# Attention values with the exponentials stationary and nine columns of v moving

## The chip, the cores and the metric

The kernel runs on one core of a Trainium2 chip. The metric is the device time of one launch in microseconds; the times given are of whole executions, and one further execution was profiled.

The engines are named as in the profile: PE is TensorE's matmul, PEld its load of the stationary operand, DVE is VectorE, ACT is ScalarE, POOL is GpSimd, SP is SyncE, which issues the DMAs.

## What is computed

Two layers run over 4 sequences of 1024 tokens with 128 features. The part that matters here is the attention of the second layer's gate branch (16 heads of 8 features, all 1024 tokens as queries and as keys):

```python
NUM_HEADS = 16                      # hd = 128 // 16 = 8
qkv = (x @ W_qkv + b_qkv).reshape(B, S, 3, H, hd)
q, k, v = (qkv[:, :, 0], qkv[:, :, 1], qkv[:, :, 2])
attn = jnp.einsum('bqhd,bkhd->bhqk', q, k) / jnp.sqrt(jnp.asarray(hd, x.dtype))
attn = jax.nn.softmax(attn, axis=-1)
attn_out = jnp.einsum('bhqk,bkhd->bqhd', attn, v).reshape(B, S, D)
...
return attn_out + moe_out
```

Beside it stand a gated feed-forward layer, a second kind of attention with a recurrence over time, a mixture of 8 experts, layer norms and a residual sum. In the kernel much of that is done in the gaps of the loop that is described next.

## The kernel before

There is one program for all engines, without loops at run time: everything is unrolled, and the order on each engine is the order in the code. Engines wait for each other through counted signals (`wait_ge`; `up` adds one). Some weights are handled by other code if they are not exactly representable; that code stands in the program and is jumped over (`t_br_lt`, `t_br`).

For each of the 4 sequences the kernel first does the first layer, then projects queries, keys and values, then runs the attention loop of `CYCLES` = 67 cycles. The loop goes over `QUADS` = 64 quads: 4 groups of four heads (`g4`), 2 halves of the queries (`c`, 512 queries each) and 8 blocks of 128 keys (`jt`, the innermost). In cycle `k_`

- PE makes the scores of quad `k_` (`m_scores`): for each of the four heads one product with 128 keys as the stationary side and 512 queries as the moving side, into four of six PSUM banks in turn;
- ACT turns them into exponentials, two heads at a time (line 1064), into `prob`, a ring of 12 slots of 512 columns in the buffer `big`. The softmax takes no maximum over the row (a bound is computed once instead);
- PE makes the values of quad `k_ - 2` (`m_values`): for each of the four heads the stationary side is `vaug`, 128 keys by 32 columns (8 features of v, a column of ones whose product is the softmax's sum, and 23 columns that belong to other heads and aren't used), the moving side the exponentials of 512 queries. The four products go to the four groups of 32 columns of the PE array and of 32 partitions in `ACC_BANK`, and are summed over the eight key blocks. The result has features in rows and queries in columns;
- PE, and after it DVE, ACT or POOL, do one side piece from the table `SIDE`: parts of the other branches. All side pieces share one PSUM bank, `SIDE_BANK`, so each waits until the one before has been read (`side_free`).

After each eighth value quad `copy_out` (DVE, line 739) copies `ACC_BANK` to `oT` in SBUF, and sets `oT_ok`, for which the values of the next eight quads wait. A side piece "nat" then transposes it on PE (four transposes of 128 x 128, line 1527) so that tokens are in rows, and `attention_out` (DVE) takes the reciprocal of the sums (line 746) and multiplies (line 748) into `att`. The last "nat", of quads 56 to 63, comes after the last values of the sequence; the sums with the experts' result (POOL, line 913), a silu (ACT, line 1099), two more operations on POOL and the store wait for it.

PE's products all have one source line, 1105 (the helper `mm`), so they are told apart by their tiles: `ps<-big,vaug` are the values, `ps<-hid` the scores, `ps<-wo_sb,qz` the side piece "o", an output projection with 32 stationary and 128 moving columns.

Of the kernel before, what the change touches and what calls it, by code (L numbers as in the profile page):

```python
# [21 lines left out]
P = 128  # L22
B, S, D = 4, 1024, 128
NT = S // P
CH = 512
# [6 lines left out]
GH = 4  # L32
# [24 lines left out]
NAT_LAST_BANK = 0  # L57
# [63 lines left out]
def build_program(nc, x, fw, lw, aw, wo, cst, cols, rows, bexp, out):  # L121
    with ExitStack() as ctx:
# [6 lines left out]
        def sig(name, per=1, start=0, left_out=0):  # L129
            return Signal(ctx, nc, name, per, start, left_out)  # L130
# [62 lines left out]
        oT = [wk[:, i * CH:(i + 1) * CH] for i in range(2)]  # L193
# [64 lines left out]
        mp_mm, oT_ok = sig("mp_mm", QUADS), sig("oT_ok", 2 * NG, 1)  # L258
        oN_mm, att_ok = sig("oN_mm", 2 * NG), sig("att_ok", 2 * NG, 1)
# [110 lines left out]
        def _(v):  # L370
# [67 lines left out]
            for b in range(B):  # L438
# [295 lines left out]
                def copy_out(n_):  # L734

                    v.wait_ge(mp_mm.sem, mp_mm.at(b, (n_ + 1) * NT))
# [25 lines left out]
                for k_ in range(CYCLES):  # L762
                    if k_ >= LAG and (k_ - LAG) % NT == NT - 1:
                        copy_out((k_ - LAG) // NT)
# [12 lines left out]
                    elif what == "nat":  # L777
                        attention_out(i)
# [145 lines left out]
        def _(a):  # L924
# [7 lines left out]
            for s_ in (chain, wblk_used, msum_ok, fin_ok, stored, z_ok, oT_ok, att_ok):  # L932
                a.sem_inc(s_.sem, s_.start)
# [169 lines left out]
        def _(t_):  # L1103
# [47 lines left out]
            for b in range(B):  # L1151
# [20 lines left out]
                t_.wait_ge(oT_ok.sem, oT_ok.at(b, 0))  # L1172
# [267 lines left out]
                def m_values(k_):  # L1440
# [7 lines left out]
                    if jt == 0 and k_:  # L1448
                        t_.wait_ge(oT_ok.sem, oT_ok.at(b, k_ // NT))
# [8 lines left out]
                def side_free(k_):  # L1458
# [5 lines left out]
                    elif what == "nat":  # L1464
                        t_.wait_ge(att_ok.sem, att_ok.at(b, i + 1))
# [19 lines left out]
                for k_ in range(CYCLES):  # L1485
# [36 lines left out]
                    elif what == "nat":  # L1522
                        side_free(k_)
                        t_.wait_ge(oT_ok.sem, oT_ok.at(b, i + 1))
# [162 lines left out]
```

## Time and profile before

| | |
|---|---|
| median of 3 runs | 1012.39 us (1012.34 to 1013.4) |
| the profiled execution | 1012.52 us, its span 1010.7 us |
| granted TensorE clock, mean | 0.996 |
| PE busy | 960.6 us, 6930 matmuls and as many loads |
| ACT busy | 746.0 us |
| DVE busy | 547.9 us |
| POOL busy | 198.5 us |
| the four attention loops | 147.1, 148.0, 148.3 and 144.7 us |

Busy time is the time in which an engine has at least one instruction under way, so four matmuls side by side count once. The end of a matmul is modelled by the profiler, its start is recorded. The loops are the stretches from 124.3, 367.1, 610.7 and 854.6 us on. The instruction queues in the profile's list of DMA queues are those over which the engines' own code arrives; q8 is PE's, as the next to last group of rows below is read.

### The profile page before, as it was taken

To read this page: it belongs to the slowest core of one execution; us is meant where nothing else is said; L and a number is where in the kernel's file an instruction comes from. 1 tells how busy PE (TensorE), PEld (TensorE's weight loads), DVE (VectorE), ACT (ScalarE), POOL (GpSimd) and SP (SyncE) were. 2 spreads that over 40 slices of the span, in tenths; PEclk is the share of its full clock that TensorE was granted. 3 is DMA by queue.
4 is the path that set the end of the run, shared out by engine and by line. 5 is a ranking of instruction groups with operands and counts; after the bars stand their busy time and mean duration, and the time that the engine had idled before them with its cause. 6 is when DMAs were issued, how large, how long until landed. Compare 5 with 4: busy or idle time off the path is not lost.

```text
span 1010.7 us, 17808 instructions
## 1 busy us (share of the span) xinstructions
PE 960.6 (95%) x6930; PEld 536.1 (53%) x6930; DVE 547.9 (54%) x1336; ACT 746.0 (74%) x914; POOL 198.5 (20%) x145
## 2 busy tenths in 40 slices
PE   3999999999899999999989999999999999999995
PEld 2888633343488853334358874334437886333431
DVE  6655735645556654554565574456447556346262
ACT  5543699989763479998956359998985446999885
POOL 1200202412300020441130020233212002035023
PEclk9999999999999999999999999999999999999998
DMA  6000133000000023200000012310000002320000
GB/s 249 1 1 1 24 48 62 1 3 1 1 22 1 2 39 50 43 2 2 1 22 1 1 17 43 51 24 2 2 1 22 1 1 26 51 35 2 2 1 23
DMA packets 17625, 22.18 MB, mean 22 GB/s; under 512 B 2976, under 2 KB 14336, under 8 KB 17280
## 3 DMA queue, kind: packets, MB, share of 16 engines
q1 hardware_dynamic: 17536, 20.99, 10.3%
q8 instruction: 57, 0.93, 0.4%
q14 instruction: 32, 0.26, 0.1%
HBM read 7.85 MB, written 2.10 MB: 10 GB/s over the span
## 4 chain that ended last, share of the span: by engine, by line
PE 76%; DVE 8%; ACT 7%; issue 6%; POOL 2%; DMA 0%; POOLq 0%; DVEq 0%; ACTq 0%
PE ps L1105 73%; ACT big L1064 3%; PE ps L1527 2%; DVE st L279 1%; ACT xn L1036 1%; DVE wk L563 1%; DVE wk L739 1%; ACT spl L1017 1%; ACT qz L1012 1%; DVE flags L420 1%; PE ps L1125 1%; DVE xn L452 1%; POOL st L877 1%; PE ps L1520 0%; DVE spl L460 0%
## 5 line engine op out<-in xcount | busy, mean ns | idle before, releaser
L1064 ACT ACTIVATE big<-ps 128x1024 f32<-128x1024 f32 x512 | 493.6, 1034 | 40.2 <-PE ps L1105 38.2
L1105 PE MATMUL ps<-big,vaug 128*32 128x512 f32 x2048 | 272.6, 604 | 3.6 <-DVE wk L739 2.3
L1105 PE MATMUL ps<-hid 32*128 32x512 f32 x1024 | 130.5, 493 | 4.3 <-ACT big L1064 2.9
L1105 PE MATMUL ps<-hid,fw_sb 128*128 128x512 f32 x416 | 101.2, 397 | 0.3 <-DVE hid L468 0.3
L980 ACT ACTIVATE wk<-ps,cols_sb 128x512 f32<-128x512 f32 x64 | 40.6, 687 | 80.2 <-PE ps L1105 74.4
L877 POOL TENSOR_TENSOR st<-st 128x4 f32<-128x4 f32 x16 | 16.2, 1010 | 389.0 <-DVE st L552 287.5
L1105 PEld LDWEIGHTS ps<-hid 32*128 32x128 f32 x1024 | 49.3, 181 | 81.5 <-issue 50.6
L891 POOL TENSOR_TENSOR qz<-qz,wk 128x512 f32<-128x512 f32 x32 | 41.2, 1288 | 244.0 <-DVE wk L709 244.0
L1105 PEld LDWEIGHTS ps<-hid,fw_sb 128*128 128x128 f32 x416 | 77.5, 188 | 18.5 <-DVE hid L468 1.1
L1105 PEld LDWEIGHTS ps<-big,vaug 128*32 128x32 f32 x2048 | 41.0, 108 | 69.6 <-issue 35.2
L727 DVE SCALAR_TENSOR_TENSOR big<-ps,sm,big 128x128 f32<-128x128 f32 x128 | 44.3, 346 | 47.0 <-PE ps L1105 35.8
L1105 PEld LDWEIGHTS ps<-wk,big 128*128 128x128 f32 x512 | 60.8, 191 | 2.1
L1105 PE MATMUL ps<-wk,big 128*128 128x129 f32 x512 | 61.0, 274 | 0.0
L1105 PE MATMUL ps<-xt_hi,lw_hi 128*128 128x512 f32 x112 | 50.7, 452 | 5.4 <-DVE wk L563 4.5
L1105 PEld LDWEIGHTS ps<-lw_hi,xt_hi 128*128 128x128 f32 x96 | 18.0, 188 | 62.4 <-DVE wk L727 34.1
L970 ACT ACTIVATE wk<-ps,cols_sb 128x512 f32<-128x512 f32 x32 | 21.9, 689 | 36.6 <-PE ps L1105 36.6
L1105 PEld LDWEIGHTS ps<-xt_hi,lw_hi 128*128 128x128 f32 x112 | 20.9, 187 | 47.9 <-issue 8.2
L696 DVE TENSOR_SCALAR wk<-ps,decay 128x512 f32<-128x512 f32 x32 | 25.9, 809 | 36.6 <-PE ps L1105 36.1
L468 DVE TENSOR_TENSOR hid<-wk,hid 128x512 fp32r<-128x512 f32 x64 | 44.3, 692 | 2.2
L1105 PE MATMUL ps<-xt_hi,lw_lo 128*128 128x512 f32 x112 | 44.2, 395 | 0.0
L466 DVE CAST hid<-wk 128x512 fp32r<-128x512 f32 x64 | 27.1, 423 | 31.6 <-ACT wk L980 30.2
L1105 PE MATMUL ps<-xt_lo,lw_hi 128*128 128x512 f32 x112 | 43.1, 396 | 0.1
(215 smaller groups left out, 1577.8 us busy)
## 6 DMA issues: line engine op xcount, KB each, us to landing
hid<-spl SPq DMA_DIRECT2D x288, 32.0 KB
xnext<-in_x SPq DMA_DIRECT2D x4, 512.0 KB, 4.0
out<-qz SPq DMA_DIRECT2D x8, 256.0 KB, 2.3
big<-in_fw SPq DMA_DIRECT2D x1, 1877.0 KB, 9.3
hid<-one_row SPq DMA_DIRECT2D x16, 96.0 KB
wk<-in_lw SPq DMA_DIRECT2D x1, 1476.0 KB, 14.2
big<-in_fw SPq DMA_DIRECT2D x1, 939.0 KB, 11.1
cst_sb<-in_cst SPq DMA_DIRECT2D x1, 440.0 KB, 4.4
```

The costliest lines, as they stand in the source:

```text
L279: step(v.bn_stats(bn[:, t, :], src[:, t, :]))
L466: up(hid_hi, v.tensor_copy(hidden(buf, 0, m), src))
L468: up(hid_lo, v.tensor_tensor(hidden(buf, 1, m), src, hidden(buf, 0, m).bitcast(F32), ALU.subtract))
L696: up(v_copy, v.tensor_scalar(v1[u % 4], ps[:, SIDE_BANK, :], decay[:, KM + m:KM + m + 1], decay[:, 2 * KM + m:2 * KM + m + 1], ALU.mult, A ...
L727: ins = v.scalar_tensor_tensor(acc, src, weight, acc, ALU.mult, ALU.add)
L877: up(rstd_ok, g_.tensor_tensor(rstd[:, tl], var[:, tl], half[:, tl], ALU.pow))
L891: up(qs_ok, g_.tensor_tensor(qz[:, m, sl], qz[:, m, sl], v1[u % 4], ALU.mult))
L970: up(l1_act, a.activation(act32[n_ % 3], ps[:, L1_BANKS[c][m % 2], :], ACT.Silu, scale=col("w1s", m)))
L980: up(h_act, a.activation(act32[n_ % 3], ps[:, banks[m], :], ACT.Gelu, scale=col(name, m)))
L1064: up(ms_exp, a.activation(prob[:, at:at + 2 * CH].rearrange("p (h n) -> p h n", n=CH), ps[:, bank:bank + 2, :], ACT.Exp, scale=HDM ** -0.5))
L1105: return t_.matmul(out_, lhsT, rhs, start=start, stop=stop, **kw)
L1527: ins = t_.transpose(ps[:, bank, q * P:(q + 1) * P], oT[i % 2][:, q * P:(q + 1) * P], ident)
```

## The change

The sides of the value product are swapped. The stationary side is now 32 queries' exponentials (128 keys by 32 columns), the moving side 9 columns of `vaug` (8 features and the ones). One quad has 4 blocks of 128 queries, 4 heads and, within a block, 4 groups of 32 queries, which go to the four column groups: 64 products where there were 4. The result lies in `ACC_BANK` with tokens in rows already, 16 pieces of 9 columns. So `copy_out`, `oT`, the eight "nat" pieces of each sequence and their bank go; `attention_out` reads `ACC_BANK` itself, at the place in DVE's order where the copy was, and what waited for `oT_ok` now waits for `att_ok`. Since the 16 pieces of a bank can't each start their own sum, four products of 32 x 144 with a stationary side of zeros set the bank to zero ahead of each eight quads.

```diff
-                    for g in range(GH):
-                        at, w = ((GH * k_ + g) % RING) * CH, (jt * HM + g4 * GH + g) * (HDM + 1)
-                        ins = mm(ps[QUAD * g:QUAD * (g + 1), ACC_BANK, :], vaug[:, w:w + QUAD], prob[:, at:at + CH],
-                                 jt == 0, jt == NT - 1)
+                        t_.wait_ge(att_ok.sem, att_ok.at(b, k_ // NT))
+                    if jt == 0:
+                        for g in range(GH):
+                            mm(ps[QUAD * g:QUAD * (g + 1), ACC_BANK, 0:TPC * GH * (HDM + 1)], vaug[:, NT * HM * (HDM + 1):],
+                               vaug[:, 0:TPC * GH * (HDM + 1)], True, False)
+                    for q in range(TPC):
+                        for h in range(GH):
+                            w, to = (jt * HM + g4 * GH + h) * (HDM + 1), (q * GH + h) * (HDM + 1)
+                            for g in range(GH):
+                                at = (GH * k_ + h) % RING * CH + q * P + QUAD * g
+                                ins = mm(ps[QUAD * g:QUAD * (g + 1), ACC_BANK, to:to + HDM + 1], prob[:, at:at + QUAD],
+                                         vaug[:, w:w + HDM + 1], False, jt == NT - 1 and q == TPC - 1 and h == GH - 1)
...
-                def copy_out(n_):
+                def attention_out(n_):
+
+                    g4, c = n_ // NCH, n_ % NCH
                     v.wait_ge(mp_mm.sem, mp_mm.at(b, (n_ + 1) * NT))
-                    if n_ == 0:
-                        v.wait_ge(hsT_mm.sem, hsT_mm.at(b, 2))
-                    up(oT_ok, v.tensor_copy(oT[n_ % 2], ps[:, ACC_BANK, :]))
-
-                def attention_out(n_):
-
-                    g4, c = n_ // NCH, n_ % NCH
-                    v.wait_ge(oN_mm.sem, oN_mm.at(b, n_ + 1))
-                    oN = ps[:, NAT_LAST_BANK if n_ == 2 * NG - 1 else SIDE_BANK, :].rearrange("p (i n) -> p i n", n=QUAD)
+                    oN = ps[:, ACC_BANK, 0:TPC * GH * (HDM + 1)].rearrange("p (i n) -> p i n", n=HDM + 1)
                     step(v.reciprocal(rec, oN[:, :, HDM]))
...
-                    elif what == "nat":
-                        side_free(k_)
-                        t_.wait_ge(oT_ok.sem, oT_ok.at(b, i + 1))
-                        bank = NAT_LAST_BANK if i == 2 * NG - 1 else SIDE_BANK
-                        for q in range(TPC):
-                            ins = t_.transpose(ps[:, bank, q * P:(q + 1) * P], oT[i % 2][:, q * P:(q + 1) * P], ident)
-                        up(oN_mm, ins)
```

On PE, around the first "nat" of a sequence (`hid` are the scores, rows with `vaug` the values, `xt_hi,lw_hi` and its like a side piece); before:

```order
L1105 MATMUL ps<-hid 128x512 x4
L1105 MATMUL ps<-big,vaug 32x512 x4
L1527 MATMUL ps<-cst_sb,wk 128x128 x4
L1105 MATMUL ps<-hid 128x512 x4
L1105 MATMUL ps<-big,vaug 32x512 x4
```

and now:

```order
L1093 MATMUL ps<-hid 128x512 x4
L1093 MATMUL ps<-vaug 32x144 x4
L1093 MATMUL ps<-vaug,big 32x9 x64
L1093 MATMUL ps<-xt_hi,lw_hi 128x512
L1093 MATMUL ps<-xt_lo,lw_hi 128x512
L1093 MATMUL ps<-xt_hi,lw_lo 128x512
L1093 MATMUL ps<-hid 128x512 x4
L1093 MATMUL ps<-vaug,big 32x9 x64
L1093 MATMUL ps<-hid 128x512 x4
```

The transposes are gone and nothing has taken their place in the table; each row of four value products has become one of 64. (PE takes each product of two float32 operands in two passes, each a load and a matmul.)

On DVE, at the first end of eight quads; before, the copy stands ahead of a side piece, and reciprocal and product follow three and more instructions later:

```order
L666 COPY sm<-ps 128x32
L739 COPY wk<-ps 128x512
L666 COPY sm<-ps 128x32
L647 TENSOR_REDUCE sm<-sm 128x8
L649 TENSOR_TENSOR sm<-sm 128x64
L696 TENSOR_SCALAR wk<-ps,decay 128x512
L746 RECIPROCAL cst_sb<-ps 128x16
L748 TENSOR_TENSOR big<-ps,cst_sb 128x4x32
```

and now both stand where the copy was:

```order
L663 COPY sm<-ps 128x32
L736 RECIPROCAL cst_sb<-ps 128x16
L738 TENSOR_TENSOR big<-ps,cst_sb 128x4x32
L663 COPY sm<-ps 128x32
L644 TENSOR_REDUCE sm<-sm 128x8
L646 TENSOR_TENSOR sm<-sm 128x64
L693 TENSOR_SCALAR wk<-ps,decay 128x512
```

The copy of 512 columns has left DVE, and the next eight quads' values wait for the product instead of for it.

## Rows read from the trace of the kernel before

**Rows 1.** The page: busy time of each engine, share of the span, instructions.

```profile
PE 960.6 (95%) x6930; PEld 536.1 (53%) x6930; DVE 547.9 (54%) x1336; ACT 746.0 (74%) x914; POOL 198.5 (20%) x145
```

**Rows 2.** Busy time by stretch (us): the four attention loops, then what lies around.

```profile
core 0: us, PE busy (x) PEld busy (x) DVE busy (x) ACT busy (x) POOL busy (x), PEclk, DMA share, GB/s
124.30:271.40 147.10, 143.91 (x1238) 55.34 (x1238) 71.50 (x196) 135.51 (x157) 33.59 (x24) 1.00 0.12 21
...
854.60:999.30 144.70, 140.89 (x1224) 53.70 (x1224) 67.01 (x176) 131.95 (x146) 31.92 (x23) 1.00 0.11 18
sum 588.10, PE 572.81 PEld 219.83 DVE 282.23 ACT 539.52 POOL 132.68; mean PE 143.20 PEld 54.96 DVE 70.56 ACT 134.88 POOL 33.17
...
999.30:1010.70 11.40, 0.63 (x4) 0.42 (x4) 1.24 (x3) 1.42 (x3) 6.22 (x5) 0.63 0.18 50
sum 422.60, PE 387.75 PEld 316.29 DVE 265.69 ACT 206.43 POOL 65.86; mean PE 77.55 PEld 63.26 DVE 53.14 ACT 41.29 POOL 13.17
```

**Rows 3.** Groups by form: count, busy us, mean ns of one, idle before and releasers.

```profile
L1064 ACT ACTIVATE big<-ps 128x1024 f32<-128x1024 f32 x512 | 493.6, 1034 | 40.2 <-PE ps L1105 38.2
L1105 PE MATMUL ps<-big,vaug 128*32 128x512 f32 x2048 | 272.6, 604 | 3.6 <-DVE wk L739 2.3 <-ACT big L1064 0.4
L1527 PE MATMUL ps<-cst_sb,wk 128*128 128x128 f32 x128 | 20.9, 286 | 4.7 <-DVE wk L739 4.7
L739 DVE COPY wk<-ps 128x512 f32<-128x512 f32 x32 | 21.9, 685 | 20.8 <-PE ps L1105 20.8
L748 DVE TENSOR_TENSOR big<-ps,cst_sb 128x128 f32<-128x128 f32 x32 | 9.3, 292 | 1.1
L746 DVE RECIPROCAL cst_sb<-ps 128x16 f32<-128x16 f32 x32 | 8.1, 254 | 25.3 <-PE ps L1527 25.3
```

**Rows 4.** Timeline of PE in the first loop: start us, us, what, count.

```profile
206.76 1.06 PE L1105 MATMUL ps<-wo_sb,qz 128*32 128x128 f32 x32
207.74 0.50 PE L1105 MATMUL ps<-hid 32*128 32x512 f32 x4
208.17 1.06 PE L1105 MATMUL ps<-big,vaug 128*32 128x512 f32 x8
209.06 1.06 PE L1105 MATMUL ps<-wo_sb,qz 128*32 128x128 f32 x32
210.04 0.51 PE L1105 MATMUL ps<-hid 32*128 32x512 f32 x4
210.48 1.07 PE L1105 MATMUL ps<-big,vaug 128*32 128x512 f32 x8
211.36 1.06 PE L1105 MATMUL ps<-wo_sb,qz 128*32 128x128 f32 x32
```

**Rows 5.** The value products by tile: duration ns min/median/max, first and last start.

```profile
L1105 PEld LDWEIGHTS ps<-big,vaug x2048: 105/108/111, 129.4 to 998.3; 128*32 128x32 f32 x187
L1105 PE MATMUL ps<-big,vaug x2048: 589/593/619, 129.4 to 998.7; 128*32 128x512 f32 x187
```

**Rows 6.** Timeline of PE's loads, one value burst.

```profile
182.53 0.19 PEld L1105 LDWEIGHTS ps<-big,vaug 128*32 128x32 f32 x8 [0.50 <-issue]
```

**Rows 7.** PE's instruction queue over the span; then DMAs from 1000.5 to 1006.5.

```profile
q8 instruction: 57, 0.93, 0.4%
...
DMA  0000040000001000000000000006100000000005
GB/s 0 0 0 0 0 109 0 0 0 0 0 0 55 0 0 0 0 0 0 0 0 0 0 0 0 0 0 109 55 0 0 0 0 0 0 0 0 0 0 154
...
q8 instruction: 2, 0.03, 2.7%
```

**Rows 8.** Timeline of all engines after the last values.

```profile
999.41 0.69 DVE L739 COPY wk<-ps 128x512 f32<-128x512 f32 x1 [6.16 <-PE ps L1105]
999.47 0.63 ACT L1099 ACTIVATE qz<-big 128x512 f32<-128x512 f32 x1
1000.22 0.42 PEld L1527 LDWEIGHTS ps<-cst_sb,wk 128*128 128x128 f32 x4 [1.85 <-issue]
1000.25 0.63 PE L1527 MATMUL ps<-cst_sb,wk 128*128 128x128 f32 x4 [0.97 <-DVE wk L739]
1000.92 0.26 DVE L746 RECIPROCAL cst_sb<-ps 128x16 f32<-128x16 f32 x1 [0.81 <-PE ps L1527]
1001.21 0.29 DVE L748 TENSOR_TENSOR big<-ps,cst_sb 128x128 f32<-128x128 f32 x1
1001.58 1.26 POOL L913 TENSOR_TENSOR big<-big 128x512 f32<-128x512 f32 x1 [4.51 <-DVE big L748]
```

More of the change, by code:

```diff
@@ L56 @@
 NORM_BANK, BOUND_BANK, VALUES_BANKS = 0, 3, (7, 7, 7)
-NAT_LAST_BANK = 0
 HEAD_ROWS = (slice(64, 80), slice(96, 112))
 SIDE = {0: ("qk", 5), 1: ("qk", 6), 2: ("mv", 1), 3: ("q", 7), 4: ("mv", 2), 5: ("k", 7), 6: ("hs", 0), 7: ("hs", 1),
[8 rows of a table removed]
[8 rows of a table added]
 CYCLES = QUADS + LAG + 1
@@ L192, in build_program @@
         moe2 = wk[:, S:2 * S].rearrange("p (t d) -> p t d", d=D)
-        oT = [wk[:, i * CH:(i + 1) * CH] for i in range(2)]
         late = cst_sb[:, CSEL:CSEL + 4 * P]
@@ L257, in build_program @@
         ms_mm, ms_exp = sig("ms_mm", 2 * QUADS), sig("ms_exp", 2 * QUADS)
-        mp_mm, oT_ok = sig("mp_mm", QUADS), sig("oT_ok", 2 * NG, 1)
-        oN_mm, att_ok = sig("oN_mm", 2 * NG), sig("att_ok", 2 * NG, 1)
+        mp_mm, att_ok = sig("mp_mm", QUADS), sig("att_ok", 2 * NG, 1)
         comb_ok, cT_mm, cT_ok, eb_mm = sig("comb_ok"), sig("cT_mm"), sig("cT_ok"), sig("eb_mm", 2)
@@ L732, in experts @@
                     v.wait_ge(ex_ok.sem, ex_ok.at(b, i + 1))
-                def copy_out(n_):
-                    v.wait_ge(mp_mm.sem, mp_mm.at(b, (n_ + 1) * NT))
-                    if n_ == 0:
-                        v.wait_ge(hsT_mm.sem, hsT_mm.at(b, 2))
-                    up(oT_ok, v.tensor_copy(oT[n_ % 2], ps[:, ACC_BANK, :]))
                 def attention_out(n_):
                     g4, c = n_ // NCH, n_ % NCH
-                    v.wait_ge(oN_mm.sem, oN_mm.at(b, n_ + 1))
-                    oN = ps[:, NAT_LAST_BANK if n_ == 2 * NG - 1 else SIDE_BANK, :].rearrange("p (i n) -> p i n", n=QUAD)
+                    v.wait_ge(mp_mm.sem, mp_mm.at(b, (n_ + 1) * NT))
+                    oN = ps[:, ACC_BANK, 0:TPC * GH * (HDM + 1)].rearrange("p (i n) -> p i n", n=HDM + 1)
                     step(v.reciprocal(rec, oN[:, :, HDM]))
@@ L763, in _ @@
                     if k_ >= LAG and (k_ - LAG) % NT == NT - 1:
-                        copy_out((k_ - LAG) // NT)
+                        attention_out((k_ - LAG) // NT)
                     what, i = side_piece(b, k_)
@@ L776, in _ @@
                             softmax8_shift(w3d(6), 0, 1, hs_sub)
-                    elif what == "nat":
-                        attention_out(i)
                     elif what == "v":
@@ L930, in normalise_next @@
                 ins.then_inc(signal, 1)
-            for s_ in (chain, wblk_used, msum_ok, fin_ok, stored, z_ok, oT_ok, att_ok):
+            for s_ in (chain, wblk_used, msum_ok, fin_ok, stored, z_ok, att_ok):
                 a.sem_inc(s_.sem, s_.start)
@@ L1171, in _ @@
                 row_scores(0)
-                t_.wait_ge(oT_ok.sem, oT_ok.at(b, 0))
+                t_.wait_ge(att_ok.sem, att_ok.at(b, 0))
                 t_.wait_ge(r_lo.sem, r_lo.at(b, 0))
@@ L1448, in m_values @@
                     if jt == 0 and k_:
-                        t_.wait_ge(oT_ok.sem, oT_ok.at(b, k_ // NT))
-                    for g in range(GH):
-                        at, w = ((GH * k_ + g) % RING) * CH, (jt * HM + g4 * GH + g) * (HDM + 1)
-                        ins = mm(ps[QUAD * g:QUAD * (g + 1), ACC_BANK, :], vaug[:, w:w + QUAD], prob[:, at:at + CH],
-                                 jt == 0, jt == NT - 1)
+                        t_.wait_ge(att_ok.sem, att_ok.at(b, k_ // NT))
[10 more added lines that the diff above has]
+                                         vaug[:, w:w + HDM + 1], False, jt == NT - 1 and q == TPC - 1 and h == GH - 1)
                     up(mp_mm, ins)
@@ L1463, in side_free @@
                         t_.wait_ge(head_in.sem, head_in.at(b, 2))
-                    elif what == "nat":
-                        t_.wait_ge(att_ok.sem, att_ok.at(b, i + 1))
                     elif what == "v":
@@ L1521, in _ @@
                         up(hs_mm, ins)
-                    elif what == "nat":
-                        side_free(k_)
-                        t_.wait_ge(oT_ok.sem, oT_ok.at(b, i + 1))
-                        bank = NAT_LAST_BANK if i == 2 * NG - 1 else SIDE_BANK
-                        for q in range(TPC):
-                            ins = t_.transpose(ps[:, bank, q * P:(q + 1) * P], oT[i % 2][:, q * P:(q + 1) * P], ident)
-                        up(oN_mm, ins)
                     elif what == "v":
```

16 rows, old and new, of the table SIDE are left out of this document.

## Prediction

> **What bounds the kernel now.** I read the page's busy shares first: PE 960.6 us (95%), ACT 746.0 us (74%), DVE 54% [rows 1]. A busy PE need not be a full one, so I cut the span into stages. Four stretches of 144.7 to 148.3 us, 588.1 us in sum, are the attention loops, one per sequence; the 422.6 us around them hold little that the change touches [rows 2]. A loop has 64 cycles with scores, so a cycle takes 588.1 / 256 = 2.30 us. In a cycle ACT makes two exponentials of 1034 ns [rows 3], 2.07 us, which leaves it 0.23 us. PE does the four score products, the values of the quad two cycles back, and a side piece. The timeline shows a cycle with no gap on PE: scores start at 207.74, values at 208.17, the side piece at 209.06, the next scores at 210.04 [rows 4]. So scores take 0.43 us, values 0.89 us, this side piece 0.98 us. PE ends last in most cycles, ACT is close behind.
>
> The profile counts 2048 value matmuls [rows 3], 8 per cycle for 4 in the code: a float32 product is a load and a matmul twice over. Its four column groups run side by side: the 8 matmuls of 604 ns each need 0.89 us, not 4.8.
>
> **The change, part by part.**
>
> 1. *The values.* The code now issues 64 products per cycle, each with 32 stationary and 9 moving columns. At two passes that is 128 loads and 128 matmuls, 256 instructions, where there were 16. What one such pair costs the trace doesn't show; it bounds it.
>  - *By columns.* Each group's pass of 512 columns takes 0.89 / 2 = 0.445 us, so 9 columns take some 8 ns: nothing.
>  - *By loads.* The first matmul of a value burst lasts 619 ns where its own load is exposed and 593 where it was hidden [rows 5]: 26 ns for 32 stationary columns. The four groups load side by side: eight loads of 108 ns begin and end within 0.19 us [rows 6]. So four pairs cost 26 ns if the next load hides under the running matmul, 26 + 8 = 34 if not. A cycle has 32 such fours: 0.83 to 1.09 us. Against 0.89 that is -0.06 to +0.20 us a cycle.
>  - *By pairs.* The nearest dense stream is the output projection (stationary 32 columns, moving 128): 32 pairs in 0.98 us [rows 4], 30.6 ns a pair. If that is the price of a pair whatever it moves, a cycle pays 128 x 30.6 = 3.92 us, +3.03.
>  - *By supply.* The cycles from 206.76 to 211.36 [rows 4] issue 88 loads and matmuls in 2.30 us, 26 ns each, sustained; the burst of [rows 6] shows the 8th load, the 15th instruction, 0.08 us behind the first, under 6 ns each, though these may have stood in a queue. Instructions come to PE in blocks by DMA: 57 packets of 16 KB on its instruction queue for 13,860 loads and matmuls [rows 1, 7], some 250 to a block (two of the 57 come after the jump below). How fast can blocks come? Only one place has PE in need of one: after its last matmul, at 1000.88, PE jumps over code that wasn't run to the program's end. In the DMA strip of that stretch (0.15 us to a slice) a block arrives in slice 5, at 1001.25, and the next in slice 27, at 1004.55: 3.3 us apart, though one takes 1.3 us to move (2.7% of 16 engines over 6.0 us, two packets) [rows 7]. It looks as if the second is not asked for until the first is in use. If a loop is fed like that, one block in hand while the next is fetched, it gets 250 instructions per 3.3 us.
>
>    A loop now has 1238 loads and as many matmuls [rows 2]; take off 1024 of the values and 56 of the transposes, add 16,384 and 128: 17,908, or 71 blocks. At 3.3 us that is 234 us per loop, 937 for four, where 588.1 stand: **+349 us**. I take this one: it is the only row that shows what happens when PE has to wait for code, and 3.66 us per cycle lies between the other bounds (2.2 and 5.3). The sustained 26 ns would give 7.3 us a cycle, but the work set that pace. Ends: if restarting after the jump is 0.7 us of the 3.3, 2.6 us a block and 738 us, +150; at 3.7, 1051 us, +463.
>
>    The Trainium skill, "Runtime: NRT & Kernel Launch", section Instruction fetch mechanics, has the sequencer fetch one 16 KiB page while it runs the current one, and holds that this hides under an issue floor of about 20 cycles per instruction; it also gives PE a memory of 2048 instructions. The 3.3 us between blocks speak for one page ahead. The floor, 17 ns if its cycles are those of 1.2 GHz, would make the 280 instructions of a cycle 4.7 us and the kernel 1610 us by an estimate; the 15 within 0.08 us don't bear it out.
>
> 2. *Clearing the bank.* Once per eight cycles four products of 144 zero columns: by the pass above 2 x 144 / 512 x 0.445 = 0.25 us, 8 per loop, 2.0 us of PE. In a loop that waits for code it hides; only in the array-bound rival does it count.
>
> 3. *Copy, transposes, their waits.* Gone are 32 copies of 685 ns on DVE and 128 transposes on PE [rows 3]. The last set of four is busy 0.63 us [rows 8], 0.29 of it the last one's own length [rows 3], so they start 0.11 us apart: 0.45 us of PE per set, seven sets per loop, 13 us in all. Like part 2 this is hidden where code is waited for. The freed bank: the next column of cycles may start its values once reciprocal (254 ns) and product (292 ns) are done, 0.55 us, where it waited for the copy, 0.69. PE's value matmuls waited 2.3 us in all for that [rows 3], so it is worth nothing. DVE has room (54%).
>
> 4. *The end of a loop.* The last copy starts at 999.41, the reciprocal at 1000.92 [rows 8]; now the reciprocal starts where the copy did, 1.51 us earlier, on the way to the sums and the store. Four times: **-6 us**.
>
> 5. *Other queues.* SP issues the same DMAs. ACT reuses a slot of the exponentials' ring once its values are done, so it falls back with PE and costs nothing itself.
>
> **Sum.** The profiled execution took 1012.52 us (span 1010.7), 0.13 above the median of 1012.39. 1012.5 + 349 - 6 = **1355 us**.
>
> **The rivals.**
>
> *A. Code arrives in time and the loads hide: faster.* The point is the price of a block: below 250 / 280 x 2.2 = 2.0 us the supply no longer sets the cycle. For it: the 1.3 us that a block takes to move, and the burst's 6 ns. Against: 3.3 us. With 26 ns per four pairs: values -0.06 x 256 = -15, clearing +8, transposes -13, ends -6: **987 us**. ACT stops this early, since 2.07 us of a cycle's 2.30 are its own; nearer 995.
>
> *B. The same, but the load stands open.* +0.20 x 256 = 51, and 8 - 13 - 6: 1052 us. At 6 ns for each of 256 instructions, none of them ready beforehand, the values take 1.54 us, and it is 1168 us. So 1015 to 1170.
>
> *C. A price per pair.* 30.6 ns each: 1012.5 + 3.03 x 256 - 6 = **1782 us**. For it: no stream in this profile goes faster for long. Against: that one moves 128 columns per product, and its four groups' time of 0.11 us is just what 128 columns cost by the 0.445 us of 512. The Trainium skill, "TensorE: Matmul & The Clock Gate", section Wait — 56ns, not 53.3ns?, states that starts of matmuls never come closer than about 25 ns however little they move. An estimate by it: 128 x 25 ns = 3.2 us of values per cycle, 1598 us. In four column groups the rows above show starts closer than that, but only in short bursts.
>
> *D. Forecast's cause, and the clock falls.* PE would stream little in 3.66 us. The granted clock is 1.00 in every loop and 0.63 only where PE stands idle at the end [rows 2]. At half speed scores (0.86), values (32 x 52 ns = 1.66) and a side piece (1.96) would make 4.5 us a cycle, above 3.66: +0.8 x 256, 1570 us at most, less where the side piece is short.
>
> **How the numbers follow.** Supply by blocks, the clock high or low (1150 to 1570): 0.45, likeliest 1355. A price per pair or per matmul (1590 to 1790): 0.20. B: 0.20. A, or within 2 us of before: 0.08. The rest, 0.07, is slower still or between the cases. About 0.2%, 2 us, is what a measurement can tell from no change here: faster 0.06, same 0.02, slower 0.92. The range leaves out A, the lower half of B and the upper part of C: 1060 to 1700.
>
> **What would show it.** Supply: cycles of 3.3 to 4 us, PE's waits put down to issue, gaps every 250 instructions, blocks on the instruction queue 3.3 us apart through the whole loop, some 300 in all. C: gaps spread evenly, starts 25 to 31 ns apart, blocks further apart than they need be. B: cycles near 2.5 us. A: values of 0.83 us and ACT without idle time. D: a granted clock near 0.5 in the loops. It would be wrong at the root if PE keeps several blocks in flight, or if the 3.3 us belong to the jump alone.

## The result: half as long again, and TensorE waiting for its own code

| | before | after |
|---|---|---|
| median | 1012.51 us (1012.34 to 1013.4) | 1492.22 us (1485.06 to 1497.16) |
| the profiled execution, its span | 1012.52, 1010.7 us | 1497.16, 1495.4 us |
| granted TensorE clock, mean | 0.996 | 0.753 |
| the four attention loops | 588.1 us [rows 2] | 1066.4 us |
| packets on PE's instruction queue | 57 [rows 7] | 297 |

The ratio of after to before is 1.473 (95%: 1.468 to 1.478). First the page of after: the busy times that answer to [rows 1], the strips of PE and of its clock over 40 slices of the span, the instruction queue, and the three costliest groups by line, which answer to [rows 3] (busy us, mean ns of one, idle time before them and what ended it).

```profile
PE 1297.0 (87%) x37778; PEld 981.9 (66%) x37778; DVE 530.4 (35%) x1304; ACT 755.2 (51%) x914; POOL 197.1 (13%) x145
...
PE   5998898778999898877999988998789997887785
...
PEclk9998655786799755578679976557768997657775
...
q8 instruction: 297, 4.87, 1.4%
...
L1052 ACT ACTIVATE big<-ps 128x1024 f32<-128x1024 f32 x512 | 495.8, 1022 | 458.0 <-PE ps L1093 455.6
L1093 PEld LDWEIGHTS ps<-vaug,big 128*32 128x32 f32 x32768 | 431.1, 138 | 237.6 <-issue 230.5
L1093 PE MATMUL ps<-vaug,big 128*32 128x9 f32 x32768 | 465.3, 194 | 135.8 <-issue 134.7
```

PE issues 37,778 pairs where it issued 6930. ACT does the same work as before (495.8 us of exponentials) but now stands idle for 458 us in front of it, waiting for PE. And PE waits too, for nothing that another engine does: "issue" is time in which the profile shows no cause. The view of waits adds these up (us in total, times, longest):

```profile
PEld ps L1093 <- issue: 385.4, 616, 2.8
...
PE ps L1093 <- issue: 162.3, 167, 2.6
```

Busy time by stretch shows where the 484.6 us between the two profiled executions lie. These are three of the four loops of after, from the first scores to the last values (the third, from 854.01, takes 266.24 us); the sum of all four answers to that of [rows 2].

```profile
124.56:388.63 264.07, 223.41 (x8953) 161.93 (x8954) 67.90 (x189) 138.41 (x157) 33.25 (x24) 0.69 0.08 15
485.40:754.28 268.88, 228.47 (x8953) 166.54 (x8954) 68.25 (x189) 139.93 (x159) 33.26 (x24) 0.66 0.08 15
...
1218.09:1485.26 267.17, 216.07 (x8940) 159.45 (x8940) 62.86 (x169) 134.59 (x147) 31.64 (x23) 0.69 0.08 13
sum 1066.36, PE 897.62 PEld 655.45 DVE 267.29 ACT 552.62 POOL 131.41; mean PE 224.41 PEld 163.86 DVE 66.82 ACT 138.16 POOL 32.85
```

A cycle now takes 1066.4 / 256 = 4.17 us. What lies around the loops takes 1495.4 - 1066.4 = 429.0 us, where the same cut through before (first scores to last values, each loop 0.6 us shorter at most than in [rows 2]) leaves 425.0. So +480.6 us in the loops, +4.0 around them.

What a single wait looks like stands in PE's timeline (start us, us, what, count, idle before), here in the first loop:

```profile
157.02 0.51 PE L1093 MATMUL ps<-hid 32*128 32x512 f32 x4
157.46 0.98 PE L1093 MATMUL ps<-vaug,big 128*32 128x9 f32 x94
160.11 0.66 PE L1093 MATMUL ps<-vaug,big 128*32 128x9 f32 x34 [1.68 <-issue]
160.70 1.12 PE L1513 MATMUL ps<-cst_sb,xn 128*128 128x128 f32 x4
161.74 0.80 PE L1093 MATMUL ps<-hid 32*128 32x512 f32 x4
```

The 128 value matmuls of one cycle break after the 94th, in the middle of a group of four, and go on 1.68 us later. No semaphore stands there, and 94 of them took only 0.98 us. In the record of the instruction queue a block of code starts to move at 157.15 and is in at 158.60; PE's first matmul behind it starts at 160.11. In each loop 69 such blocks arrive, one every 264.1 / 69 = 3.83 to 268.9 / 69 = 3.90 us; for the first loop the list of queues has (packets, MB, share of 16 engines)

```profile
q8 instruction: 69, 1.13, 1.8%
```

Within one block, four pairs of load and matmul for the four column groups start 30 to 31 ns apart at the full clock (2.4 GHz) and 52 to 53 ns apart at the half (1.2 GHz), so a cycle's 128 pairs would need 1.0 us, against the 0.89 of before.

So the reading before any experiment: the array could do the new values nearly as fast as the old ones, but the code for them doesn't arrive.

### The profile page after: what moved, and what is told of

The parts are those of the page before. It is cut to its first block, busy times and chain, and to the rows that moved or that the text cites. A ratio compares the mean times of both kernels' runs of the same rounds, so it can differ in the third digit from the quotient of the medians.

```text
span 1495.4 us, 79426 instructions
## 1 busy us (share of the span) xinstructions
PE 1297.0 (87%) x37778; PEld 981.9 (66%) x37778; DVE 530.4 (35%) x1304; ACT 755.2 (51%) x914; POOL 197.1 (13%) x145
## 4 chain that ended last, share of the span: by engine, by line
PE 80%; issue 14%; DVE 3%; ACT 2%; POOL 1%; DMA 0%; POOLq 0%; DVEq 0%
PE ps L1093 78%; DVE wk L560 1%; PE ps L1513 0%; ACT spl L1005 0%; ACT qz L1000 0%; DVE st L276 0%; DVE flags L417 0%; PE ps L1113 0%; PE ps L1567 0%; DMA xnext<-in_x 0%; DVE xres L507 0%; DVE wk L502 0%; ACT qz L916 0%; DVE hid L465 0%; POOL big L901 0%
## 5 line engine op out<-in xcount | busy, mean ns | idle before, releaser
L1052 ACT ACTIVATE big<-ps 128x1024 f32<-128x1024 f32 x512 | 495.8, 1022 | 458.0 <-PE ps L1093 455.6
L1093 PEld LDWEIGHTS ps<-vaug,big 128*32 128x32 f32 x32768 | 431.1, 138 | 237.6 <-issue 230.5
L1093 PE MATMUL ps<-vaug,big 128*32 128x9 f32 x32768 | 465.3, 194 | 135.8 <-issue 134.7
L1093 PE MATMUL ps<-hid 32*128 32x512 f32 x1024 | 188.3, 664 | 5.5 <-issue 5.0
L1093 PEld LDWEIGHTS ps<-hid 32*128 32x128 f32 x1024 | 71.1, 242 | 109.3 <-issue 103.4
L968 ACT ACTIVATE wk<-ps,cols_sb 128x512 f32<-128x512 f32 x64 | 40.5, 687 | 80.2 <-PE ps L1093 74.4
L1093 PE MATMUL ps<-wo_sb,qz 128*32 128x128 f32 x1024 | 50.7, 341 | 16.6 <-issue 16.6
L1093 PE MATMUL ps<-xt_hi,lw_hi 128*128 128x512 f32 x112 | 59.5, 531 | 4.9 <-DVE wk L560 4.5
L1093 PE MATMUL ps<-lw_hi,xt_hi 128*128 128x512 f32 (+1 forms) x96 | 53.0, 552 | 2.2 <-issue 2.2
L1093 PE MATMUL ps<-xt_lo,lw_hi 128*128 128x512 f32 x112 | 50.2, 459 | 1.5 <-issue 1.4
L1093 PEld LDWEIGHTS ps<-wo_sb,qz 128*32 128x32 f32 x1024 | 38.1, 138 | 17.0 <-issue 16.7
```

The lines of the kernel that those rows point to most:

```text
L968: up(h_act, a.activation(act32[n_ % 3], ps[:, banks[m], :], ACT.Gelu, scale=col(name, m)))
L1052: up(ms_exp, a.activation(prob[:, at:at + 2 * CH].rearrange("p (h n) -> p h n", n=CH), ps[:, bank:bank + 2, :], ACT.Exp, scale=HDM ** -0.5))
L1093: return t_.matmul(out_, lhsT, rhs, start=start, stop=stop, **kw)
```

## The experiments

The theory: in code that runs straight through, PE (its loads and matmuls together) is handed a block of 256 instructions every 3.4 to 3.9 us whatever is in it, and the number of instructions sets the time. The rivals: a price of each pair of load and matmul (25 to 31 ns, C), and the fallen clock (D).

**Fewer products.** e1_half computes the values of two of the four heads, e2_threeq those of three (the softmax's sums of the others are replaced, so the output isn't the attention's):

```diff
-                        for h in range(GH):
+                        for h in range(2):        # e2_threeq: range(3)
...
-                    step(v.reciprocal(rec, oN[:, :, HDM]))
+                    step(v.reciprocal(rec, (oN[:, 0:1, HDM]).broadcast_to([P, TPC * GH])))
```

> Leaves out the value products of two of each group's four heads (their outputs are wrong), so a quad has 32 products instead of 64. Supply theory (a block of 256 PE instructions every 3.85 us, whatever is in it): a loop has 17,931 - 8192 = 9739 instructions, 38 blocks, 147 us of supply; that is no longer above what PE and ACT need, so the loops fall to 147 to 160 us and the kernel to 1000 to 1060 us, with few waits put down to issue. Price per pair (each load and matmul costs the same everywhere): the values of the changed kernel cost 1492 - 1012 + 228 = 708 us in all, half of them go, 1138 us. Clock theory (the halved clock is what costs): as the price per pair.

> Leaves out one of each group's four heads (wrong outputs), 48 products to a quad. Supply: 17,931 - 4096 = 13,835 instructions per loop, 54 blocks at 3.85 us = 208 us where 266.5 stand, 1492 - 4 x 58 = 1259 us, blocks still 3.7 to 3.9 us apart. Price per pair: a quarter of 708 us goes, 1315 us, and the blocks come further apart only as the work asks. The two kernels with fewer products together: by supply the first quarter is worth 233 us and the second 200 to 260; by price both 177.

Measured: 1064.92 and 1288.79 us. The first lies 5 us above what supply expected and 73 below the price per pair, the second in the middle of the two. Counted by loops: in e1_half 37 or 38 blocks arrive in 156.7 to 163.3 us, 4.2 to 4.4 us apart, further apart than in after, so code is no longer the only limit there (a cycle is 2.5 us, near the 2.3 that ACT and PE need in any case). In e2_threeq 53 blocks come in 212 to 221 us, 4.0 to 4.2 apart. But the size of the step speaks for nobody: the third quarter of the products costs 224 us and the last 203, for 8192 pairs each, 27 and 25 ns a pair. A price per pair of 25 ns would explain those two numbers just as well. It needed other runs.

**More columns per product.** e3_wide32 moves 32 columns of v where after moves 9; the number of instructions is the same (the clearing of the bank is 64 columns wider too, and the overlap of the columns spoils the output):

```diff
-                                ins = mm(ps[QUAD * g:QUAD * (g + 1), ACC_BANK, to:to + HDM + 1], prob[:, at:at + QUAD],
-                                         vaug[:, w:w + HDM + 1], ...
+                                ins = mm(ps[QUAD * g:QUAD * (g + 1), ACC_BANK, to:to + 32], prob[:, at:at + QUAD],
+                                         vaug[:, w:w + 32], ...
```

> All 64 products, but each moves 32 columns instead of 9 (sums are wrong where they overlap): the same number of instructions, 3.6 times the columns. Supply: the same time, 1480 to 1510 us, since four pairs then cost at most 30 to 60 ns, still below what a block's wait allows. Clock theory: the granted clock rises above 0.75 with more columns streamed, and the time falls with it, by 50 us or more. Price per column: slower, by 23 x 64 x 256 x 2 passes at the half clock, over 100 us.

Measured: 1487.96 us, at a granted clock of 0.917 where after has 0.753. The strip of the clock, PE's waits over the span (162.3 us of this kind in after), and the timeline of a stretch in the first loop:

```profile
PEclk9999888889999999999999998899979998888896
...
PE ps L1093 <- issue: 297.5, 239, 2.6
```

```profile
203.01 1.20 PE L1093 MATMUL ps<-vaug,big 128*32 128x32 f32 x116
205.83 0.32 PE L1093 MATMUL ps<-vaug,big 128*32 128x32 f32 x12 [1.62 <-issue]
```

The clock rises and the time stays within 0.3%: the loops take 266.0 to 269.3 us, 69 blocks each. Over the four loops PE is busy for 761.5 us where after has 897.6: what the work got back from the clock became waiting. In the stretch shown 116 matmuls run in 1.20 us and then PE waits 1.62. At the half clock the same stretch of after has only a short wait, since the work fills the time between two blocks:

```profile
205.85 1.78 PE L1093 MATMUL ps<-vaug,big 128*32 128x9 f32 x116
207.90 0.39 PE L1093 MATMUL ps<-vaug,big 128*32 128x9 f32 x12 [0.27 <-issue]
```

So the clock is a consequence here and not a cause; what it takes from the work it takes from the wait.

**The operations by themselves.** e4_micro is a kernel of its own that does none of the reference's work: long streams of products of one form, with no other engine in the loop. The forms are, in this order, 9 moving columns in float32, 128 columns in float32, 9 columns with 128 stationary ones, 9 columns in bfloat16 (one pass, so no second load), then a loop at run time whose body is 112 pairs of load and matmul, and last 9 columns in one column group alone.

> No layer at all, the output is the input: PE alone runs streams of products one after the other, with nothing to wait for. First 32 of 128 x 200 (to wake the clock), then 512 float32 products of 32 stationary and 9 moving columns in four column groups (2048 instructions, 8 blocks), 512 with 128 moving columns, 96 with 128 stationary and 9 moving, 1024 bfloat16 ones of 32 and 9 (one pass each, 2048 instructions), then a loop at run time of 56 such float32 products (10 columns, 224 instructions) run 16 times, and 256 in one column group alone. Supply: every straight stream that needs a block in less than about 3.4 us gets one each 3.3 to 3.8 us, so the 9-column stream takes 27 to 30 us and the bfloat16 one the same; inside a block four pairs take 30 ns (60 at the half clock); the loop at run time, whose code is already there, runs at that pace throughout, 16 x 112 pairs in 14 us (28 at the half clock), and no block arrives in it. Price per pair: loop and straight code alike, evenly spaced, 25 to 31 ns a pair.

Its timeline of PE, with lines of each form:

```profile
30.66 1.25 PE L158 MATMUL ps<-va,pr 128*32 128x9 f32 x128 [2.19 <-issue]
34.11 1.89 PE L158 MATMUL ps<-va,pr 128*32 128x9 f32 x128 [2.21 <-issue]
37.56 1.89 PE L158 MATMUL ps<-va,pr 128*32 128x9 f32 x128 [1.56 <-issue]
41.29 1.90 PE L158 MATMUL ps<-va,pr 128*32 128x9 f32 x128 [1.84 <-issue]
...
67.12 3.72 PE L158 MATMUL ps<-va,pr 128*32 128x128 f32 x128 [0.29 <-issue]
...
131.48 1.19 PE L158 MATMUL ps<-vab,prb 128*32 128x9 bf16 x128 [2.26 <-issue]
135.21 1.19 PE L158 MATMUL ps<-vab,prb 128*32 128x9 bf16 x128 [2.54 <-issue]
...
153.66 53.82 PE L158 MATMUL ps<-va,pr 128*32 128x10 f32 x2211 [2.38 <-issue]
```

Bursts of exactly 128 matmuls, which with their loads are 256 instructions, begin 3.45 or 3.73 us apart. Whether a burst is busy for 1.25 us (full clock) or 1.89 us (half), in float32 or bfloat16, the next begins at the same distance. The 128-column stream, whose 128 matmuls are busy for 3.72 us, hardly waits (0.29 us). The last row is the loop (1697 of the 2211 matmuls, until 179.0 us) and the stream in one column group behind it, without a break between. From the third on, the loop's 16 passes of 112 pairs take 1.66 to 1.67 us each, 14.9 ns a pair at the half clock. A last block moves over the instruction queue from 156.24 to 157.20 us, and then none until 184.66: the last 13 passes run without one. Nearly the same pairs (10 columns for 9) that cost 27 ns each in straight code (3.45 / 128) cost 15 in a loop. That is what a price per pair can't do: 27 ns is the spacing of blocks divided by 128.

The starts in this trace also show why a block's content doesn't matter as long as it is short. For all 14 bursts that begin behind a wait, a transfer takes 0.88 to 1.30 us, PE's first matmul follows 1.25 to 1.54 us after its end, and the next transfer begins 1.03 to 1.20 us after that matmul. The three add up to the 3.45 or 3.73 us from burst to burst. So the next block isn't asked for until the one before is in use, as the prediction had guessed from two blocks.

**The same products with less code.** In e5_loop 48 of a cycle's 64 value products are three passes of a loop at run time over the same 16, in the kernel itself (constant addresses, and the reciprocal as in e1_half, so the output isn't the attention's):

```diff
-                    for q in range(TPC):
+                    def block_of(q, last):
                         for h in range(GH):
...
+                        return ins
+
+                    with t_.Fori(0, TPC - 1):
+                        block_of(0, False)
+                    ins = block_of(TPC - 1, jt == NT - 1)
```

> PE executes the same 64 products a quad, but 48 of them come from a loop at run time: the 16 products of the first 128 queries are run three times, the last 16 once (the middle two blocks' sums are therefore wrong). Executed loads and matmuls as in the changed kernel, plus three branches; code to fetch about 155 instructions a cycle instead of 280. Supply theory: 0.62 blocks of 3.85 us is 2.4 us a cycle, so the work itself sets the pace: scores 0.43, values 32 x 31 ns and three branches of 0.21, a side piece of 0.9, 3.0 us a cycle at full clock, up to 3.7 where the clock is halved: 1190 to 1370 us. Price per executed pair: 1492 us or, with the branches, 1650.

Measured: 1254.42 us, 238 less than after, with the same 37,778 loads and matmuls executed. The packets on the instruction queue fall from 297 to 172:

```profile
q8 instruction: 172, 2.82, 1.0%
```

A loop's 38 or 39 blocks come 5.2 to 5.8 us apart, so code no longer sets the pace. What does? The timeline from 500 us on, at the full clock:

```profile
502.03 1.79 PE L1093 MATMUL ps<-vaug,big 128*32 128x9 f32 x128
503.75 0.50 PE L1093 MATMUL ps<-sel_r,pick 16*128 16x512 f32 x1
```

The values take 1.72 us a cycle (502.03 to the next start at 503.75), not 1.0. The comparisons at the end of the three passes are recorded 0.50 us apart, and a pass of eight groups of four pairs explains 8 x 31 ns = 0.25 us of that. I put the other 0.25 us down to the jump back, and tested that: in e9_loop2 two passes over 28 products, and 8 behind them.

```diff
-                    with t_.Fori(0, TPC - 1):
-                        block_of(0, False)
-                    ins = block_of(TPC - 1, jt == NT - 1)
+                    with t_.Fori(0, 2):
+                        products(0, 7, False)
+                    ins = products(14, 2, jt == NT - 1)
```

> The run-time loop of e5_loop, cut otherwise: 56 of a cycle's 64 value products come from two passes through the code of 28 (addresses constant, so the output is not the attention's), 8 stand behind it. Executed products and passes are those of e5_loop; the passes through the loop are two where they were three, the code to be fetched is 36 products where it was 32. In e5_loop one pass at full clock takes 0.50 us, of which its eight groups of four pairs explain 8 x 31 ns = 0.25; the other 0.25 us I put down to the jump back. Theory (the jump's price): one jump less per cycle, 256 x 0.25 = 64 us less than e5_loop's 1254 us: 1190, between 1175 and 1205. Rival 1 (the time of e5_loop's values lies in its instructions, however they are looped): 1254, nothing changes. Rival 2 (blocks of code still set the pace in e5_loop): four more products to fetch per cycle, 16 x 256 instructions = 16 blocks of 3.84 us, 61 us more: 1315.

Measured: 1198.71 us, 55.7 us less than e5_loop, where the theory had 64. It looks like a hit, but the two kernels didn't run at the same clock: 0.931 on average in e5_loop, 0.977 in e9_loop2. Busy time by stretch, first and fourth loop, of e5_loop and then of e9_loop2:

```profile
124.20:343.60 219.40, 211.31 (x8953) 154.35 (x8954) 67.99 (x189) 138.72 (x157) 33.36 (x24) 0.81 0.09 16
...
1045.70:1242.50 196.80, 182.88 (x8939) 132.60 (x8940) 62.61 (x169) 134.12 (x147) 31.79 (x23) 1.00 0.09 15
```

```profile
123.97:324.00 200.03, 189.87 (x8951) 138.96 (x8954) 67.75 (x189) 137.96 (x157) 33.43 (x24) 0.91 0.10 18
...
997.56:1186.80 189.24, 176.40 (x8939) 129.55 (x8940) 62.52 (x169) 134.05 (x147) 31.82 (x23) 1.00 0.10 16
```

The second loops take 198.4 us (clock 1.00) and 196.6 (0.98), the third 220.9 (0.81) and 194.3 (1.00). So 46 of the 55.4 us by which the loops differ lie in the first and the third, where e5_loop's clock had fallen; in the two where both kernels had nearly the full clock it is 1.8 and 7.6 us. The same place as above, in e9_loop2:

```profile
502.28 1.75 PE L1093 MATMUL ps<-vaug,big 128*32 128x9 f32 x128
503.95 0.49 PE L1093 MATMUL ps<-sel_r,pick 16*128 16x512 f32 x1
```

The values take 1.67 us here, 0.05 less than in e5_loop. Over all cycles whose values ran at the full clock the medians are 1.70 us (243 cycles) and 1.78 (211). One jump less is worth 0.05 to 0.07 us a cycle, 13 to 18 us in all, where the theory had 0.25 and 64; that the time fell into the theory's range was luck, most of it the clock's. The starts of matmuls show where the theory was wrong. Inside a pass a group of four follows 11 or 12 ns after the last start of the one before, as a rule. Behind the two jumps back of the cycle shown of e5_loop it follows after 222 and 240 ns, behind the third pass, which doesn't jump, after 102; behind the one jump of e9_loop2's cycle it takes 313 ns. So a jump has no fixed price, and the one that stayed became dearer. Why stays open, and so does why the clock fell further in e5_loop. The rival by which blocks still set the pace (1315 us) is out: 42 or 43 blocks per loop come 4.5 to 4.7 us apart.

**Half the instructions, all the work.** e6_onepass keeps all 64 products of after, but holds the exponentials and v in bfloat16, so that a product is one pass, one load and one matmul.

```diff
-        vaug = sb("vaug", [P, NT * HM * (HDM + 1) + QUAD])
+        vaug = sb("vaug", [P, NT * HM * (HDM + 1) + QUAD], BF)
...
-        prob = big[:, :, :, :].rearrange("p a g n -> p (a g n)")[:, 0:RING * CH]
+        prob = big[:, :, :, :].rearrange("p a g n -> p (a g n)").bitcast(BF)[:, 0:RING * CH]
```

> The changed kernel with exponentials and v in bfloat16 for this product (less precise): each product is one load and one matmul instead of two and two. All 64 products are made. Supply: 17,931 - 8192 - 64 = 9675 instructions a loop, 38 blocks as in the kernel with half of the products: 1040 to 1070 us. Price per product rather than per instruction: near 1492. Price per executed pair: 1138.

Measured: 1069.3 us. It does what e1_half does, which has as many pairs (9674 and 9738 instructions per loop) for half the products: 1069 and 1065. The time follows instructions, not products. That alone would fit a price per executed pair too (1138 expected, missed by 69), but together with e5_loop it doesn't.

**The other side of the change.** e7_no_nat keeps before's value products and takes the rest of the change: no copy, no transposes, the ends of eight quads where after has them (the multiplication then reads the bank in the wrong layout, so the output isn't the attention's).

> The kernel before with its own value products (4 a quad), and of the change only the rest: no copy, no transposes; reciprocal and product read the bank as it lies (outputs are wrong). Forecast from the prediction's parts 3 and 4: -6 us for the ends of the four loops, and up to -13 us for the 28 sets of transposes where PE sets the pace: 993 to 1006 us. A rival: ACT is so close behind PE in the loop that only the ends count, 1004 to 1007 us.

Measured: 997.17 us, ratio 0.985 (95%: 0.983 to 0.987), 15.4 us less than the 1012.53 of before beside it. Busy time by stretch, its loops and then what lies behind them (94.72, 95.07, 94.79 and 10.56 us):

```profile
124.39:268.57 144.18, 139.65 (x1210) 52.50 (x1210) 66.75 (x188) 134.06 (x156) 33.54 (x24) 1.00 0.12 21
...
sum 575.97, PE 555.58 PEld 208.31 DVE 263.27 ACT 533.78 POOL 132.67; mean PE 138.90 PEld 52.08 DVE 65.82 ACT 133.45 POOL 33.17
```

```profile
268.57:363.29 94.72, 93.98 (x494) 76.21 (x486) 61.14 (x130) 48.40 (x72) 13.97 (x10) 1.00 0.06 11
...
984.94:995.50 10.56, 0.60 (x8) 0.00 (x0) 0.55 (x2) 2.04 (x3) 6.23 (x5) 0.70 0.19 54
```

By the same cut before has 585.7 us in the loops, then 96.3, 96.2, 96.2 and 12.0. So the transposes and their waits are worth 9.7 us in the loops, and the earlier end 1.6 + 1.1 + 1.4 + 1.4 = 5.5 us. That is the whole gain that the change could have had if its products had cost what the old ones did.

**Old side, one pass.** e8_before_onepass is the kernel before with the exponentials and v in bfloat16, the same two lines as in e6_onepass.

> The kernel before with exponentials and v in bfloat16 for this product (less precise), order and counts of products unchanged: one pass of each of the four instead of two, at one step per column. Values of a cycle fall from 0.89 to about 0.22 us, PE's cycle to 1.65 us, so ACT with two exponentials of 1.034 us sets the pace of most cycles at 2.1 to 2.2 us: 256 x 0.1 to 0.2 = 25 to 50 us less, 960 to 990 us. If PE's float32 values didn't matter (ACT bound all along): 1010.

Measured: 1011.97 us (1000.67 to 1015.12), ratio 0.997 (0.994 to 1.000), 22 us above the upper end of what was expected. The values' array time is halved, and nothing comes of it. Its loops, their sum, then the stretch behind the first:

```profile
124.49:270.89 146.40, 127.26 (x981) 58.52 (x982) 71.84 (x195) 133.18 (x155) 33.30 (x24) 0.81 0.12 20
...
sum 577.22, PE 499.86 PEld 228.07 DVE 283.76 ACT 528.51 POOL 131.54; mean PE 124.97 PEld 57.02 DVE 70.94 ACT 132.13 POOL 32.89
```

```profile
270.89:371.45 100.56, 98.50 (x494) 80.61 (x493) 62.33 (x131) 48.65 (x72) 13.90 (x10) 0.94 0.06 10
```

The loops gave 8.5 us (585.7 to 577.2), at a clock of 0.81 to 0.83, and the three stretches between them took 10 back (100.6, 97.6 and 100.5 us where before has 96.3, 96.2 and 96.2), at a clock of 0.94 to 0.97 where before has 1.00. Inside the loops two things nearly cancel. Here are eight cycles of the first loop and then six others, of e8_before_onepass:

```profile
137.21:153.12 15.91, 13.34 (x114) 5.72 (x114) 8.32 (x27) 15.91 (x21) 0.00 (x0) 1.00 0.29 46
160.82:176.10 15.28, 15.28 (x74) 4.94 (x75) 6.74 (x10) 13.30 (x15) 5.79 (x5) 0.50 0.36 71
```

and the same cycles of before:

```profile
138.45:156.03 17.58, 17.58 (x147) 6.42 (x146) 8.29 (x27) 16.54 (x21) 0.00 (x0) 1.00 0.32 50
162.62:175.45 12.83, 12.75 (x98) 3.70 (x99) 6.63 (x10) 12.44 (x15) 5.14 (x4) 1.00 0.39 79
```

At the full clock the eight cycles take 1.99 us each instead of 2.20, and now ACT is busy throughout. At the half clock the six take 2.55 instead of 2.14, and PE is busy throughout. Counted over 252 cycles (from scores to the next scores), 163 had the full clock and take 2.08 us where they took 2.30, with ACT idle for 0.06 us of it; that is the limit and the gain that were expected, 35 us in sum. The other 89 had the half clock for all or part of their time and take 2.44 us where they took 2.15, 26 us more. So the fallen clock, which the expectation left out, took back nearly all of the gain in the loops and the rest behind them. The ten executions point the same way: the fastest (1000.67 us) has the highest clock, 0.904, the slowest (1015.12) the lowest, 0.877.

## Why the prediction was right where it was, and what was mis-sized

*What bounds the kernel.* Right: PE in nearly every cycle, ACT 0.2 us behind. How close ACT is e8_before_onepass showed: with the values' array time halved a cycle at the full clock still took 2.08 us, and ACT was idle for 0.06 of it.

*Part 1, the values.* The mechanism taken, code by blocks, is what the runs show. The count was right too: 17,908 loads and matmuls and 71 blocks per loop foretold, 17,907 and 69 found (17,931 with PE's waits and signals). The mis-sized term is the price of a block: 3.3 us taken, read off one place where PE had jumped to the end of the program, 3.83 to 3.90 measured over whole loops. 4 x 69 x 3.86 = 1066 us where the sum had 937: 129 of the 142 us by which the profiled execution (1497.16 us) lies above the forecast. Another 2 us are where the loops were cut ([rows 2] against first scores to last values). The price was even above the end of 3.7 that the text allowed for it, so the sum's own upper end (+463) was passed. The time lies in the range given to supply (1150 to 1570) only because that range also covered a price for the fallen clock, which e3_wide32 shows not to be there; that part is luck, and so wide a range (1060 to 1700 in all) asks little of the number. Why 3.86: where nothing else is in the way (e4_micro) a block takes 3.45 or 3.73 us from one start to the next; in the loops of after the 272 distances between block starts run from 3.25 to 5.69 us, 3.77 on average, so 3.3 was the low end of them. The rest up to 3.86 are the ends: a loop's first block comes 6.6 to 8.1 us after its first scores, its last one 2.5 to 3.5 us before the end. Why 3.45 in one place and 3.73 in another stays open.

"Runtime: NRT & Kernel Launch" in the Trainium skill, section Instruction fetch mechanics, calls the crossing of a 16 KiB block "mostly hidden". It also warns that a jump to code outside a window of two such pages stalls, and gives that as one reason why kernels prefer full unrolling. This case's traces agree with blocks of 256 instructions and with one block ahead. They disagree with the hiding: crossings cost 1.56 to 2.54 us in e4_micro. The warning itself isn't tested, since the loops here (64 to 224 instructions) are shorter than a block, but for these short instructions unrolling is the slower way: the kernel with jumps (1198.71 us) is 294 us faster than the unrolled one.

*Part 2, clearing the bank.* Foretold as hidden; no run shows it by itself.

*Part 3, copy and transposes.* Up to 13 us foretold for a kernel bound by the array; e7_no_nat gives 9.7 in the loops. That it is hidden in after was argued and has no run of its own.

*Part 4, the end of a loop.* 1.51 us foretold for each, 1.1 to 1.6 in e7_no_nat. In after only the last of the four shows it (10.1 us from the last values to the end, before 12.0). The timeline there:

```profile
1485.08 0.39 PE L1093 MATMUL ps<-vaug,big 128*32 128x9 f32 x10 [1.57 <-issue]
```

```profile
1485.57 0.26 DVE L736 RECIPROCAL cst_sb<-ps 128x16 f32<-128x16 f32 x1 [17.65 <-PE ps L1093]
1485.86 0.29 DVE L738 TENSOR_TENSOR big<-ps,cst_sb 128x128 f32<-128x128 f32 x1
```

Reciprocal and product follow the last value at once, without the copy and the transposes of [rows 8]. Behind the other three loops the clock is granted at 0.93 to 0.97 in place of 1.00, and those stretches are 0.5, 3.5 and 1.6 us longer than before, not 1.5 shorter. That is the other 10 us of the miss, and no part of the sum had it.

*The rivals.* A (987 us) and B (1052) needed code in time. Their picture of the array was right, with a size between the two: four pairs in 31 ns, values of 1.0 us a cycle. By that +0.11 x 256 = 28 us, +8 for clearing the bank and -15 for e7_no_nat's part, the change would take some 1033 us if code were free; this is an estimate for the full clock, and no run shows it. But a block costs 3.86 us, not below the 2.0 that A asked for. C's price of 25 to 30 ns per pair (1598 and 1782) can be read off the time itself (e1_half to e2_threeq to after), and it is only 3.45 us over 128. The floor of 25 ns between starts of matmuls in the Trainium skill ("TensorE: Matmul & The Clock Gate", section Wait — 56ns, not 53.3ns?) doesn't hold across four column groups: 7.7 ns a pair here, sustained for a whole block. D's sign came (a clock of 0.65 to 0.69 in the loops), its price didn't: the half clock makes values of 1.7 us out of 1.0 and scores of 0.73 (202.57 to 203.30 in after's trace) out of 0.44 (157.02 to 157.46), and all of it fits into the wait for code, as e3_wide32 shows. Where D computed 4.5 us for a cycle at the half clock throughout, the clock kept coming back.

*What would show it.* Waits put down to issue, bursts broken after some 250 instructions and some 300 blocks (297): all found. The foretold cycle of 3.3 to 4 us was 4.17, the blocks 3.77 us apart and not 3.3.

## What to carry to other kernels

Count instructions, not only columns: code that runs straight through came to PE at 256 instructions per 3.4 to 3.9 us, some 13 to 15 ns each, so a load and matmul pair shorter than about 27 ns per issue (over all column groups) waits for its code. The sign is a burst that breaks after 128 pairs with idle time put down to issue, while more columns or a higher clock change nothing; what helps is fewer instructions, or a short loop at run time if its jumps (0.22 to 0.31 us from the last start before to the first behind, at the full clock) cost less than the code that they save. Before speeding up one engine, ask how close the next one is, and look at the clock afterwards: halving the values' array time of the old kernel left at most 0.2 us a cycle to gain before ACT, and the fallen clock took that back. And before two times are compared, compare the granted clocks: most of the step from e5_loop to e9_loop2 was the clock.

## What the runs showed of the hardware that was not expected

- Of the 3.77 us between the starts of two blocks less than a third is bytes moving (1.1 us at the median in after). At 157.15 us it was 1.45 us of transfer, and 1.5 more until PE's first instruction from the block. The next one isn't under way meanwhile: in e4_micro it begins 1.03 to 1.20 us after PE's first matmul from the block before, although PE has nothing to do for 1.6 to 2.5 us between two blocks.
- Code inside a loop at run time wasn't fetched again: no block in the last 13 of the 16 passes of e4_micro's loop, whose body is 112 pairs.
- The pause at a jump back has no fixed length: 222 and 240 ns between two starts in e5_loop, 313 in e9_loop2, both at the full clock, and 187 (where 53 is usual) in e4_micro at the half clock.
- The mean granted clock was 0.753 with 9 moving columns, 0.917 with 32 and the same instructions, 0.879 for the old kernel with one pass and 0.996 with two. The fallen clock cost nothing where code set the pace, and in e8_before_onepass 26 us in 89 cycles of the loops and 10 in the dense stretches behind them.
